# Attention over 1601 keys: scores in two runs a batch instead of seven groups of tiles, projections and mixing in one go behind each run

## The reference, cut to what matters

```python
Q = (x_q @ W_Q + b_Q).reshape(B, L, H, dk).transpose(0, 2, 1, 3)      # B 32, L 64, H 16, dk 16
K = (x_k @ W_K + b_K).reshape(B, S, H, dk).transpose(0, 2, 1, 3)      # S 1601
V = (x_v @ W_V + b_V).reshape(B, S, H, dk).transpose(0, 2, 1, 3)
scores = jnp.einsum('bhld,bhsd->bhls', Q, K) / jnp.sqrt(jnp.float32(dk))
attn = jax.nn.softmax(scores, axis=-1)
ctx = jnp.einsum('bhls,bhsd->bhld', attn, V)
```

## Time and profile before

| | us |
|---|---|
| median of 3 runs (2275.38 to 2279.4) | 2278.74 |
| the profiled execution's own time | 2274.29 |
| its span, first to last instruction | 2272.6 |
| TensorE matmuls busy, whole span (28,676 matmuls, as many weight loads) | 2104.7 (93%) |
| VectorE busy | 1431.4 (63%) |
| ScalarE busy | 1248.1 (55%) |
| GpSimd busy | 746.8 (33%) |

### The profile page before, as it was taken

One profiled execution on the slowest core, in us unless ns is written; L12 is line 12 of the kernel. 1 busy time (PEld: TensorE's weight loads), 2 busy tenths in 40 slices (PEclk: granted clock), 3 DMA queues, 4 the chain that ended last, 5 costly groups with the idle time before them and its releaser, 6 DMA issues. The chain is left out here.

```text
span 2272.6 us, 65088 instructions
## 1 busy us (share of the span) xinstructions
PE 2104.7 (93%) x28676; PEld 1739.0 (77%) x28676; DVE 1431.4 (63%) x2619; ACT 1248.1 (55%) x1680; POOL 746.8 (33%) x571
## 2 busy tenths in 40 slices
PE   7999999999999999999999999789599998599993
PEld 5888889999999999999989988644133237599993
DVE  6555555555555555555555554446788884788885
ACT  3455555555555555555555555258799981366661
POOL 2222232232232222222222220000699972255541
PEclk9999999999999999999999999899899999699997
DMA  3111111111111111111111110214875430766663
GB/s 108 46 43 41 42 49 41 42 50 41 41 50 40 42 48 43 38 46 41 40 48 43 40 42 7 67 45 150 234 175 145 139 93 17 233 225 219 229 232 125
DMA packets 131138, 195.41 MB, mean 86 GB/s; under 512 B 18116, under 2 KB 109252, under 8 KB 130696
## 3 DMA queue, kind: packets, MB, share of 16 engines
q1 hardware_dynamic: 121832, 174.98, 25.8%
q0 software_dynamic: 4416, 12.06, 1.6%
q10 hardware_dynamic: 4608, 4.20, 0.5%
HBM read 159.61 MB, written 31.59 MB: 84 GB/s over the span
## 5 line engine op out<-in xcount | busy, mean ns | idle before, releaser
L560 DVE TENSOR_REDUCE max_part<-work 128x1 f32<-128x384 f32 (+1 forms) x1024 | 535.2, 569 | 174.4 <-PE work L688 150.5
L623 ACT ACTIVATE probs<-scores 128x1024 f32<-128x1024 f32 (+1 forms) x416 | 424.0, 1026 | 331.7 <-PE scores L713 320.2
L235 POOL TENSOR_TENSOR ctx_lo<-ctx_whole,ctx_hi 128x768 fp32r<-128x768 f32 (+1 forms) x128 | 231.7, 1811 | 992.8 <-DVE ctx_hi L229 992.8
L555 DVE SCALAR_TENSOR_TENSOR keys_lo<-work,bk,keys_hi 128x384 fp32r<-128x384 f32 (+1 forms) x256 | 162.7, 635 | 329.2 <-ACT keys_hi L602 329.2
L1332 POOL TENSOR_TENSOR decay<-steps_in,xn 128x1024 f32<-128x1024 f32 x126 | 243.4, 1965 | 133.8 <-POOLq L940 116.2
L707 PE MATMUL scores<-q_hi,keys_hi 64*128 64x256 f32 (+1 forms) x1664 | 252.0, 282 | 1.7 <-issue 1.0
L707 PE MATMUL scores<-q_hi,keys_lo 64*128 64x256 f32 (+1 forms) x1664 | 248.7, 278 | 1.3 <-issue 1.3
L707 PE MATMUL scores<-q_lo,keys_hi 64*128 64x256 f32 (+1 forms) x1664 | 248.8, 278 | 0.6 <-issue 0.6
L678 PE MATMUL work<-wv_hi,ctx_hi 128*128 128x256 f32 (+1 forms) x832 | 244.0, 293 | 0.2
L678 PE MATMUL work<-wv_hi,ctx_lo 128*128 128x256 f32 (+1 forms) x832 | 234.1, 281 | 0.0
L678 PE MATMUL work<-wv_lo,ctx_hi 128*128 128x256 f32 (+1 forms) x832 | 233.9, 281 | 0.0
(11 more groups left out here) (233 smaller groups left out, 4582.7 us busy)
## 6 DMA issues: line engine op xcount, KB each, us to landing
xs<-in_w_T SPq DMA_DIRECT2D x46, 1024.0 KB, 7.3
ctx_whole<-in_ctx_T SPq DMA_DIRECT2D x96, 384.0 KB, 3.3
steps_in<-scratch_results SPq DMA_DIRECT2D x256, 128.0 KB, 2.8
ctx_whole<-in_ctx_T SPq DMA_DIRECT2D x32, 449.0 KB, 3.4
scratch_results<-steps SPq DMA_DIRECT2D x16, 512.0 KB, 2.6
scratch_mixed<-mixed ACTq DMA_DIRECT2D x32, 128.0 KB, 3.2
scratch_z<-z SPq DMA_DIRECT2D x16, 256.0 KB, 3.7
zg<-scratch_z SPq DMA_DIRECT2D x16, 256.0 KB, 3.3
```

Source lines behind the costliest of these rows:

```text
L235: nc.gpsimd.tensor_tensor(s.ctx_lo[c][:, :, 0:n], s.ctx_whole[c % 2][:, :, 0:n], s.ctx_hi[c][:, :, 0:n].bitcast(F32), ALU.subtract).then_i ...
L555: nc.vector.scalar_tensor_tensor(keys_lo[par][:, m, start:start + n], bank[:, 0:n], s.bk[:, m:m + 1], keys_hi[par][:, m, start:start + n]. ...
L560: nc.vector.reduce_max(max_part[par][:, place(pair), c:c + 1], bank[:, 0:CHUNKS[c][1]], AX) \
L623: nc.scalar.activation(probs[n % PROBS][0:rows, :], scores[slot][0:rows, :], ACT.Exp, scale=1.0 / HD ** 0.5).then_inc(exp_done, 1)
```

## The change

The 13 tiles are scored in two runs, tiles 0 to 6 and 7 to 12. Between the scores of a run lie maxima units only: 14 in the first run and 2 behind it, 16 in the second (of which four lie before tile 9 and four before tile 11). All keys and values units stand behind the runs, and behind them all the run's tiles are mixed, 7 and then 6. The units of chunks 0 and 1 of the keys and of values 0 and 1 (FIRST_UNITS) become the first units of a batch and are worked off one batch earlier: behind the row unit of batch b + 1 follow those of batch b + 2, and then the mixing of batch b's second run. The buffers of probabilities become 7. GpSimd makes the masked queries of batch b before the last chunk's split and waits for the scores of batch b - 2 instead of its mixing.

```diff
-PAIRS_OF_TILES = [
-    ([0, 1], [[], []],
-     keys_unit(0, 0) + keys_unit(1, 0) + values_unit(0, 1)),
-    ([2, 3], [maxima(0, 0, 2), maxima(0, 2, 4)],
-     maxima(0, 4, 6) + keys_unit(0, 1) + keys_unit(1, 1) + values_unit(2)),
-    ([4, 5], [maxima(0, 6, 8), maxima(1, 0, 2)],
-     maxima(1, 2, 4) + keys_unit(0, 2) + keys_unit(1, 2) + values_unit(3, 4)),
-    ([6, 7], [maxima(1, 4, 6), maxima(1, 6, 8)],
-     maxima(2, 0, 2) + keys_unit(0, 3) + keys_unit(1, 3) + values_unit(5)),
-    ([8, 9], [maxima(2, 2, 4), maxima(2, 4, 6)],
-     maxima(2, 6, 8) + values_unit(6, 7) + values_unit(8)),
-    ([10, 11], [maxima(3, 0, 2), maxima(3, 2, 4)],
-     maxima(3, 4, 6) + values_unit(9, 10)),
-    ([12], [maxima(3, 6, 8)],
-     values_unit(11, 12) + [("row",)]),
-]
-UNITS = [unit for tiles, before, after in PAIRS_OF_TILES for unit in sum(before, []) + after]
+FIRST_UNITS = keys_unit(0, 0) + keys_unit(1, 0) + keys_unit(0, 1) + keys_unit(1, 1) + values_unit(0, 1)
+PHASES = [
+    ([0, 1, 2, 3, 4, 5, 6],
+     [maxima(0, 0, 2), maxima(0, 2, 4), maxima(0, 4, 6), maxima(0, 6, 8), maxima(1, 0, 2), maxima(1, 2, 4),
+      maxima(1, 4, 6)],
+     maxima(1, 6, 8) + keys_unit(0, 2) + keys_unit(1, 2) + values_unit(2) + values_unit(3, 4) + keys_unit(0, 3)
+     + keys_unit(1, 3) + values_unit(5) + values_unit(6, 7)),
+    ([7, 8, 9, 10, 11, 12],
+     [maxima(2, 0, 2), maxima(2, 2, 4), maxima(2, 4, 6) + maxima(2, 6, 8), maxima(3, 0, 2),
+      maxima(3, 2, 4) + maxima(3, 4, 6), maxima(3, 6, 8)],
+     values_unit(8) + values_unit(9, 10) + values_unit(11, 12) + [("row",)]),
+]
+UNITS = FIRST_UNITS + [unit for tiles, before, after in PHASES for unit in sum(before, []) + after]
...
-MIXED_BEHIND = {3: [0, 1, 2, 3], 7: [4, 5, 6, 7], 12: [8, 9, 10, 11, 12]}
-PROBS = 5
+PROBS = 7
...
-            def prepare(b, par, more=True):
-                pool.wait_ge(lo_split, (b + 1) * NC)
-                if b >= 1:
-                    pool.wait_ge(probs_used, (b - 1) * NT + PROBS)
-                    mask_queries(nc, pool, s, b, par)
-                if more:
-                    for c in range(NC):
-                        split(b + 1, c)
+            def mask(b):
+                if b >= 2:
+                    pool.wait_ge(scores_ready, (b - 1) * NT)
+                mask_queries(nc, pool, s, b, b % 2)
...
+            for b in range(2, batches):
+                for c in range(NC - 1):
+                    split(b, c)
+                mask(b)
+                split(b, NC - 1)
...
+            def first_units(b, par):
+                for u in range(len(FIRST_UNITS)):
+                    unit(b, par, u)
...
-                    for t in MIXED_BEHIND.get(tiles[-1], []):
+                    if tiles[-1] == NT - 1 and b + 2 < batches:
+                        first_units(b + 2, par)
+                    for t in tiles:
                         mix(b, par, t)
...
             for u in range(NU):
                 unit(0, 0, u)
+            first_units(1, 1)
             for b in range(batches):
-                attend(b, b % 2, b + 1 < batches)
+                attend(b, b % 2)
```

More of the change, by code:

```diff
@@ L434 @@
 BESIDE = []
-upto = 0
-for tiles, before, after in PAIRS_OF_TILES:
+upto = len(FIRST_UNITS)
+for tiles, before, after in PHASES:
     places = []
@@ L514, in split @@
                 low_part(nc, pool, s, b, c)
-            def prepare(b, par, more=True):
-                pool.wait_ge(lo_split, (b + 1) * NC)
-                if b >= 1:
-                    pool.wait_ge(probs_used, (b - 1) * NT + PROBS)
-                    mask_queries(nc, pool, s, b, par)
-                if more:
-                    for c in range(NC):
-                        split(b + 1, c)
-            for c in range(EARLY, NC):
-                split(0, c)
+            def mask(b):
+                if b >= 2:
+                    pool.wait_ge(scores_ready, (b - 1) * NT)
+                mask_queries(nc, pool, s, b, b % 2)
             def add_bias(first, last):
@@ L530, in add_bias @@
                     nc.gpsimd.tensor_tensor(s.x_tok[:, t, :], s.x_tok[:, t, :], s.bo[:, :], ALU.add)
[L532 to L535, removed]
+            for c in range(EARLY, NC):
+                split(0, c)
+            mask(1)
+            for c in range(NC):
+                split(1, c)
+            for b in range(2, batches):
[3 more added lines that the diff above has]
+                split(b, NC - 1)
+                if b < 2 + LN_GROUPS:
                     add_bias((b - 2) * GT, (b - 1) * GT)
@@ L613, in unit, with attend @@
                         .then_inc(unit_copied, 1)
-            def attend(b, par, ahead):
+            def first_units(b, par):
+                for u in range(len(FIRST_UNITS)):
+                    unit(b, par, u)
+            def attend(b, par):
                 for tiles, before, after in BESIDE:
@@ L624, in attend @@
                                              scale=1.0 / HD ** 0.5).then_inc(exp_done, 1)
-                    if ahead:
+                    if b + 1 < batches:
                         for u in after:
                             unit(b + 1, 1 - par, u)
+                if b + 2 < batches:
+                    first_units(b + 2, par)
                 act.wait_ge(probs_used, b * NT + NT + PROBS)
```

## The result

The changed kernel takes 2356.89 us (median of 4 runs, 2355.25 to 2357.95), the kernel before beside it on the same chip 2278.79 us: a ratio of 1.0342, 95% interval 1.0327 to 1.0356. Its profiled execution took 2356.57 us with a span of 2354.8 us, against 2272.6 us of before: 82.2 us more, on the same clock (0.968 against 0.969). One of the four executions of a_short took 4068.02 us, far from all others, and is left out of the figures for that run.

The account below looks back on a forecast made before the run. TensorE was taken as the bound, busy 43.17 of 44.55 us a batch. The terms -73 + 46 + 41 + 48 = +62 us gave 2336 on the profiled execution, forecast 2337 us, range 2292 to 2368.

Parts of the forecast that it names:

- Part 1: TensorE's changes between kinds of matmul in attention: fewer of them save 2.3 us a batch, -73 us in all.
- score loop: Two score buffers in a run of seven tiles: 2.23 us against 2.24 us of TensorE, taken as 0 without slack.
- Part 2: Maxima bunched in the second run wait for VectorE's reductions through three PSUM banks: 1.48 us a batch, +46 us.
- Part 3: Keys right behind the row wait for VectorE's shifts with nothing beside it: 1.32 us a batch, +41 us.
- Part 4: Longer mixing blocks: TensorE halts when a whole instruction packet lies inside one, 1.25 packets a batch, +48 us.
- rival A: Instruction fetch keeps up, so longer mixing blocks cost no more than now: +14, 2290 us; chance 12%.
- The rest: Score buffers, probability buffers, GpSimd's masking, context loads, first and last batch: together taken as 0.
- rival D: Score buffers tip (16 us) and packet edges stay in both mixing blocks (+75 instead of +48): 2379 us; chance 9%.
- the ends: First batch's projections with 16 maxima in a row, last batch with fewer waits: 0 with 5 us either way.
- The other signs: Batches without halt 43.2 us apart, TensorE idle 1.3 us between row and keys, halts in mixing of 50 to 75 us.

Follow-up runs that it names:

- a_short: The changed kernel with mixing in blocks of three and four tiles, then three ahead of the row unit and three at the end: 2299.54 us.
- b_kind: The kernel before with three pairs of maxima moved from ahead of two keys units to between them: 2408.71 us.
- b_kind_single: The kernel before with one maximum of each of three pairs moved between the two keys units behind them: 2327.17 us.
- b_maxcols: The kernel before with VectorE's reductions reading 64 columns of each maximum: 2253.79 us.
- a_maxcols: The changed kernel with VectorE's reductions reading 64 columns of each maximum instead of 384 or 449: 2321.96 us.
- a_best: a_row with the maxima spread: 16 in the first run, two behind values 6-7, 14 in the second, two or three a tile: 2311.92 us.
- a_comb: a_short_row with two pairs of maxima moved beside the first run's mixing, so exactly two a tile in both runs: 2231.03 us.
- a_row: The changed kernel with the second run's six tiles mixed between the row unit and the next first units: 2322.77 us.
- a_short_row: a_short with its three early tiles of the second run mixed behind the row unit instead of ahead of it: 2266.54 us.
- b_longmix: The kernel before with its mixing in two blocks of seven and six tiles and seven buffers of probabilities: 2333.45 us.
- a_phase: The changed kernel with tiny matmuls ahead of value units, making each later batch 6 packets of instructions long: 2318.44 us.

## Why the prediction was right, point by point

2357 us lies in the range and the sign was the likeliest, but the forecast (2337) was 20 us short. By its own steps:

- **Part 1 (-2.3 us a batch).** The views and the prices hold: a pair of changes costs 0.31 to 0.51 us by b_kind and b_kind_single, where 0.44 was taken, and b_maxcols shows that those gaps are not VectorE's, against the name of their releaser. The gaps ahead of keys and values fell from 62.1 us in 215 to 18.6 us in 62. The whole saving was not measured alone. It follows from the undisturbed batch: +0.90 us is 1.43 (row) + 1.56 (maxima) + 0.22 (score loop) less the saving, which gives 2.3. Some of that may not be changes of kind: b_maxcols took 0.39 us a batch off the kernel before that VectorE had held up among its scores and maxima. If the longer runs took the same off, the changes alone are worth 1.9 us, an estimate from these figures.
- **Part 2 (+1.48).** Measured 1.56 (48.3/31), in the second run as forecast. The explanation was too narrow: reductions at 0.22 us still leave 29.7 of the 48.3 us (a_maxcols). Spreading over the same tiles moves it (a_best), two a tile remove it (a_comb). The Trainium skill warns in "TensorEngine Tiling (Array Packing)", section PSUM Bottleneck, that the copying out of PSUM may become the bottleneck. The waits of 48.3 us agree with it only in part, since reductions less than half as long took away 18.6 of them.
- **Part 3 (+1.32).** Measured 1.43 by the steps (1.65 us from row to keys, 0.22 of it the row itself), 43.7 us of waits against 41, in 30 waits where 31 had been counted; a_row and a_short_row take it away by putting mixing there.
- **Part 4 (+48).** Measured +46.5 us in the 29 periods. The reading of it stood up to three tests: halts come with longer blocks alone (b_longmix), go with shorter ones (a_short), and go with the same blocks once the edges stand elsewhere (a_phase). That the size fits so well is partly luck. The prediction had 1.25 halts a batch of 1.6 us each, 40 in all; the view has 47 gaps of 1.2 us in the mean. For the kernel before it had 8 of 1.6 us, and the view has 18 of 0.9. The Trainium skill, in "Runtime: NRT & Kernel Launch", section Instruction fetch mechanics, calls the crossing of an edge mostly hidden; in this code the 57 us of halts decide against it, and rival A is out.
- **The rest (0).** This is where the forecast was short, in two terms. The first is the score loop: 2.23 us against 2.24 was taken as fitting, with the tip left to rival D. It does tip, by 0.22 us a batch, 7 us in 31, where five late steps a batch, 16 us, had been priced. The second is the ends, put at 0 within 5 us, which cost 10.1 - 1.3 = 8.8 us, some of it halts. The first batch bears the 10.1, about 6 of it the five units brought forward. The last batch was to have fewer waits, but takes 23.9 us instead of 20.8. A halt of 1.58 us lies in its mixing, and its scores, with no unit between them, take 1.4 us more; with exponentials of 896 columns the last batch takes 21.9 us.
- **The sum.** In a form like that of the prediction: 31 batches by 0.90 instead of 0.50 is +28 instead of +15.5 (+7 score loop, +3 row, +2.5 maxima), halts +46.5 instead of +48, ends and the rest 8 instead of -2: 82 instead of 62.

The other signs came as told: best batches of 43.67 us (43.2 foretold), 1.27 us idle ahead of the keys, halts of 57 us (50 to 75) in up to two places a batch. What was not foretold is that the two runs are not at fault themselves: with its three costs covered, the arrangement is 2.0% faster than the kernel before (a_comb), though covering them gives back some of the changes of kind that were saved.

## What to carry to other kernels

Before work is gathered into longer runs, list what the interruptions were hiding: a producer's latency (row to shifts), the turn of a few PSUM banks, and here even the fetching of instructions, since small matmuls issued 14 ns apart use up a packet in 1.78 us, faster than the next one arrived. Then keep the long runs but put the dense block into those gaps in pieces no longer than a packet of instructions (192 and 256 in a_short_row). A loop that fits with 0.01 us to spare should be priced as one that doesn't.

## What was new about the hardware here

- A halt for instructions depends on where the packet edge falls: 36 tiny matmuls at the start and 4 or 5 a batch took the halts from 57.0 to 7.6 us and made a kernel with more instructions 38 us faster. All halts of over 0.4 us in the attention stages of both kernels, 14 in before and 49 in after, end at one place, the remainders 193 to 195, counting TensorE's traced instructions by 256.
- A change from a maximum (64 rows) to keys (128 rows) left TensorE's weight loads idle for 0.21 us and one back for 0.27 us (b_kind_single); from values to maxima, the first step is only 0.09 us longer. The profile may put a releaser's name on such a gap that has nothing to do with it, as max_part in before (b_maxcols).
- With three banks in turn, a unit shares its bank with the third one behind it: a keys unit with two maxima between it and the one before waited 0.95 to 1.3 us (b_kind), since its bank goes through ScalarE and VectorE one after the other.
